# Layer 0 of a two-layer graph network on one core: h2 in a PSUM bank, and the one-hot's transposes in one bank with one copy

## The reference

```python
def _L0_gnn_ref(x, edge_index, W1, b1, W2, b2):
    x_i, x_j = x[dst], x[src]
    msg_in = jnp.concatenate([x_i, x_j - x_i], axis=-1)
    h = jax.nn.leaky_relu(msg_in @ W1 + b1, 0.01)
    h = jax.nn.leaky_relu(h @ W2 + b2, 0.01)
    return jax.ops.segment_sum(h, dst, num_segments=x.shape[0])
...
x = _layernorm(x + _L0_gnn_ref(x, edge_index, ...), axis=-1)
x = _layernorm(x + _L1_gnn_ref(x, edge_index, ...), axis=-1)   # graph attention, 4 heads
```

## Time and profile before

| | |
|---|---|
| median of 3 runs | 8842.36 us (8837.32 to 8854.7) |
| the profiled execution's own time | 8853.59 us |
| its span (first to last instruction) | 8851.8 us |
| busy: PE, PEld, DVE, ACT, POOL | 5979.6, 4612.0, 5775.0, 3918.0, 6098.9 us |
| gathers of layer 0 (3136), first to last start | 87.2 to 4055.2 us |
| gathers of layer 1 (3136), first to last start | 4222.3 to 8582.6 us |
| mean granted clock of TensorE | 0.888 of full |

### The profile page before, as it was taken

The page is one execution under the profiler, slowest core; times in us unless marked ns, Lnnn a source line. Parts: engine busy times, 40 slices in busy tenths (PEclk is TensorE's granted clock), DMA queues, the critical chain, the costliest instruction groups (busy, mean ns, idle before and its releaser), DMA issues.

```text
span 8851.8 us, 202989 instructions
## 1 busy us (share of the span) xinstructions
PE 5979.6 (68%) x46823; PEld 4612.0 (52%) x46824; DVE 5775.0 (65%) x13889; ACT 3918.0 (44%) x10077; POOL 6098.9 (69%) x6281
## 2 busy tenths in 40 slices
PE   4777777777777777776366666666666666666667
PEld 3556555555555555555244445444444444444446
DVE  3555555555555555556477777777777777777776
ACT  3445444544444444444244444444444444444443
POOL 4777777777777777772777776767676766766650
PEclk7889888988988888888698989999898989999897
DMA  3111111111111111112111111111111111111110
GB/s 99 40 40 40 39 40 40 40 40 40 39 40 40 40 40 40 40 40 30 27 29 30 28 28 26 28 27 28 27 27 27 27 28 26 27 28 27 27 21 15
DMA packets 276883, 301.80 MB, mean 34 GB/s; under 512 B 169511, under 2 KB 173108, under 8 KB 276566
## 3 DMA queue, kind: packets, MB, share of 16 engines
q0 software_dynamic: 200704, 265.33, 14.7%
q1 hardware_dynamic: 74082, 32.92, 1.5%
q10 hardware_dynamic: 2068, 3.20, 0.1%
HBM read 286.33 MB, written 16.30 MB: 34 GB/s over the span
## 4 chain that ended last, share of the span: by engine, by line
DVE 25%; issue 22%; POOL 21%; PE 18%; DVEq 6%; ACT 4%; ACTq 2%; POOLq 1%; DMA 1%; SPq 0%
POOL big L382 21%; DVE S L485 8%; PE ps L970 6%; PE pu L956 4%; DVE state L684 2%; DVE rel L482 2%; PE ps L846 2%; DVE rowA L633 1%; DVE rowD L638 1%; POOLq L373 1%; DVE Y L665 1%; DVEq L256 1%; DVEq L700 1%; ACT rowX L1087 1%; ACT ST L1174 1%
## 5 line engine op out<-in xcount | busy, mean ns | idle before, releaser
L382 POOL DMA_INDIRECT big<-x_dram,idx x3136 | 3084.8, 984 | 1442.5 <-issue 892.7
L382 POOL DMA_INDIRECT big<-q_dram,idx x3136 | 3013.0, 961 | 1041.2 <-issue 1033.9
L956 PE MATMUL pu<-Y,S 128*128 128x265 f32 x7856 | 2147.5, 418 | 738.2 <-DVE Y L665 732.5
L956 PEld LDWEIGHTS pu<-Y,S 128*128 128x128 f32 x7856 | 1497.5, 201 | 1030.8 <-issue 782.2
L665 DVE TENSOR_TENSOR Y<-big,ps 128x1040 f32<-128x1040 f32 x982 | 1210.7, 1233 | 659.0 <-ACT ps L1178 572.5
L485 DVE TENSOR_TENSOR S<-ps,rel 128x1024 f32 x978 | 1197.8, 1225 | 222.1 <-DVE rel L482 222.1
L1075 ACT COPY ST<-ps 128x512 bf16<-128x512 bf16 x978 | 538.8, 586 | 1703.7 <-PE ps L846 1703.6
L860 PE MATMUL pu<-rowX,S 128*128 128x192 bf16 x3936 | 578.0, 264 | 980.4 <-issue 718.6
L522 DVE TENSOR_TENSOR Y<-Y,rowX 128x512 f32<-128x512 f32 x491 | 341.7, 696 | 1221.3 <-ACT rowX L1087 1218.9
L860 PEld LDWEIGHTS pu<-rowX,S 128*128 x3936 | 383.7, 98 | 1174.7 <-issue 1063.5
L970 PE MATMUL ps<-identb,S 128*128 128x128 bf16 x3912 | 550.3, 231 | 523.9 <-DVE S L485 522.7
(11 more groups left out here) (176 smaller groups left out, 8322.6 us busy)
## 6 DMA issues: line engine op xcount, KB each, us to landing
big<-q_dram,idx POOLq DMA_INDIRECT x3136
big<-x_dram,idx POOLq DMA_INDIRECT x3136
rowD<-dst_dram SPq DMA_DIRECT2D x196, 32.0 KB
x_dram<-big SPq DMA_DIRECT2D x7, 483.0 KB, 6.1
idx<-srcT_dram SPq DMA_DIRECT2D x98, 32.0 KB, 1.7
dstc<-dstT_dram SPq DMA_DIRECT2D x98, 32.0 KB
q_dram<-state SPq DMA_DIRECT2D x2, 1536.0 KB, 9.6
out<-big SPq DMA_DIRECT2D x6, 448.0 KB
```

Source lines behind the costliest of these rows:

```text
L382: nc.gpsimd.indirect_dma_start(o, None, x_dram if l else q_dram, bass.IndirectOffsetOnAxis(ap=idx[:, half, t:t + 1], axis=0)).then_inc(gat ...
L956: last = t_.matmul(bank, Sf[:, t, :], Y[:, t, :], start=(t == 0), stop=(t == 7))
```

## The change

`h2` becomes the view `ps[1][:, :]`, a whole PSUM bank of 128 x 512 float32, in place of a quarter of `Y`. `h2`, `hi`, `rest`, `mid` and `lo` address it there. To free the bank, the 8 transposes of the one-hot go to `ps[0]` (8 x 128 columns of bf16 fill it), with one pair of semaphores `stp`, `sts` instead of two, and ACT moves them to `ST` in one copy of 128 x 1024 instead of two of 128 x 512. PE waits for the whole copy before z0. DVE gets a wait on its own `lo` ahead of the write of `h2`, and in the prologue a wait for the index rows' copies (`rc`) and one more memset of a bank. Layer 1's turn calls the helper `to_sbuf` for the copy that it had written out.

```diff
--- before.py
+++ after.py
@@ -140,7 +140,7 @@
         h1 = Yf[:, 0:TG * D].rearrange("p (t d) -> p t d", d=D)
         az1 = Yf[:, TG * D:2 * TG * D].rearrange("p (t d) -> p t d", d=D)
         az2 = Yf[:, 2 * TG * D:3 * TG * D]
-        h2 = Yf[:, 3 * TG * D:4 * TG * D]
+        h2 = ps[1][:, :]
         h2p = rowX[:, 0:3 * TG * D // 2].bitcast(bf16).rearrange("p (k c) -> p k c", k=3)
         h1T = rowA[:, 0:4 * P].rearrange("p (t e) -> p t e", e=P)
         Sf = S[:, 2 * TG:4 * TG, :].rearrange("p t n -> p (t n)").bitcast(f32).rearrange("p (t n) -> p t n", n=P)
@@ -164,7 +164,7 @@
         fredge_flatd = sem("fredge_flatd")
         gdone = sem("gdone")
 
-        LAGS = [{"rel": 0, "S": 0, "stp0": 0, "stp1": 0, "sts0": 0, "sts1": 0, "z0": 0, "z1": 0, "az0": 0,
+        LAGS = [{"rel": 0, "S": 0, "stp": 0, "sts": 0, "z0": 0, "z1": 0, "az0": 0,
                  "az1": 0, "h0": 1, "h1": 1, "htp": 1, "hts": 1, "z2": 1, "az2": 1,
                  "h2": 2, "hi": 2, "rest": 2, "mid": 2, "lo": 3, "U": 3, "us": 4, "acc": 4},
                 {"rel": 0, "S": 0, "stp": 0, "sts": 0, "ad": 0, "adx": 1, "zz": 1,
@@ -517,6 +517,7 @@
                                             hv(az1, h), ALU.max).then_inc(m[f"h{h}"], 1)
                     if k.has(2):
                         k.after("az2", 2)
+                        k.after("lo", 3)
                         v.tensor_tensor(h2, ps[7][:, :], az2, ALU.max).then_inc(m["h2"], 1)
                         k.after("hi", 2)
                         v.tensor_tensor(h2, h2, h2p[:, 0, :], ALU.subtract).then_inc(m["rest"], 1)
@@ -533,7 +534,8 @@
 
             prime(dve, 0, "rel S h0 h1 h2 rest lo us acc")
             dve.sem_inc(fredge_flatd, 2)
-            for n in (2, 4, 5, 6, 7):
+            dve.wait_ge(s["rc"], 2 * NU)
+            for n in (1, 2, 4, 5, 6, 7):
                 link(v.memset(ps[n][:, :], 0.0))
             link(v.memset(rowX[:, :], 0.0))
             dve.wait_ge(s["b2in"], 16)
@@ -838,13 +840,12 @@
 
             def transposes(k, buf):
                 k.after("S", 0)
+                k.after("sts", 1)
                 hot = S[:, ds(buf, TG), :]
-                for h in range(2):
-                    k.after(f"sts{h}", 1)
-                    o = ps[h][:, 0:2 * P].bitcast(bf16)
-                    for t in range(4):
-                        last = t_.transpose(o[:, t * P:t * P + P], hot[:, h * 4 + t, :], identb[:, :])
-                    last.then_inc(L[k.l][f"stp{h}"], 1)
+                o = ps[0][:, :].bitcast(bf16)
+                for t in range(TG):
+                    last = t_.transpose(o[:, t * P:t * P + P], hot[:, t, :], identb[:, :])
+                last.then_inc(L[k.l]["stp"], 1)
 
 
             def turn0(half):
@@ -872,8 +873,8 @@
                                                     .rearrange("p t d -> p (t d)"), ident[:, :])
                         last.then_inc(m["htp"], 1)
                     if k.has(0):
+                        k.after("sts", 0)
                         for h in range(2):
-                            k.after(f"sts{h}", 0)
                             for j in range(3):
                                 t_.matmul(ps[4 + h][:, 0:256], identb[:, :],
                                           g0[:, ds(k.r * TG + (half * TS + 4 * h), 4), j, :], start=(j == 0),
@@ -904,7 +905,7 @@
 
             pe.wait_ge(s["b2in"], 16)
             pe.wait_ge(s["idb"], 1)
-            prime(pe, 0, "stp0 stp1 htp z0 z1 U z2")
+            prime(pe, 0, "stp htp z0 z1 U z2")
             pe.sem_inc(gdone, 2)
             pe.wait_ge(clean, 1)
             supers(pe, steps0)
@@ -1070,11 +1071,9 @@
 
             def to_sbuf(k):
 
-                for h in range(2):
-                    k.after(f"stp{h}", 0)
-                    a_.copy(ST[:, h * 4:h * 4 + 4, :],
-                            ps[h][:, 0:2 * P].bitcast(bf16).rearrange("p (t n) -> p t n", t=4)
-                            ).then_inc(L[k.l][f"sts{h}"], 1)
+                k.after("stp", 0)
+                a_.copy(ST[:, :, :], ps[0][:, :].bitcast(bf16).rearrange("p (t n) -> p t n", t=TG)
+                        ).then_inc(L[k.l]["sts"], 1)
 
 
             def turn0(k):
@@ -1106,7 +1105,7 @@
             def steps0(i, q, half):
                 steps(act, 0, i, first0, turn0)
 
-            prime(act, 0, "sts0 sts1 hts az0 az1 az2 hi mid")
+            prime(act, 0, "sts hts az0 az1 az2 hi mid")
             act.wait_ge(clean, 1)
             supers(act, steps0)
             tails(act, 0, turn0)
@@ -1170,9 +1169,7 @@
                     if k.has(1):
                         ends(k, 0, 1)
                     if k.has(0):
-                        k.after("stp", 0)
-                        a_.copy(ST[:, :, :], ps[0][:, :].bitcast(bf16).rearrange("p (t n) -> p t n", t=TG)
-                                ).then_inc(m["sts"], 1)
+                        to_sbuf(k)
                     if k.has(1):
                         k.after("y1", 2)
                         a_.activation(wb[:, :, :], dw[:, :, :], ACT.Exp).then_inc(m["w"], 1)
```

## The result

The changed kernel takes 8792.2 us (median of 6 runs, 8788.54 to 8796.38) against 8842.79 us for the kernel before in the same comparison (6 runs, 8833.76 to 8854.7): ratio **0.9942**, 95% interval 0.9931 to 0.9953, or 50.6 us less. The forecast was 8800 us. The profiled execution took 8796.38 us, with a span of 8794.5 us; it is the one read here.

The account below looks back on a forecast made before the run. POOL's stream of gathers, not the turn, was taken to bound layer 0. Terms -46.2 + 1 + 3.0 = -42 us, against the median of 8842.36 us, gave 8800 us; range 8780 to 8830.

Parts of the forecast that it names:

- What bounds layer 0: In layer 0 POOL issues gathers end to end and PE waits 706.9 us, so only shortening POOL's stream counts.
- Which gathers are held, and by what (-46.2): Layer 0 gathers starting in `lo` or `rest` wait because both inputs lie in SBUF; `h2` in PSUM saves 46.2 us.
- held by the memset: One of the 167 long gathers began in a prologue memset, counted as held by it for 0.15 us.
- Rival A: Layer 0 holds stay, perhaps from `lo`'s bf16 write into `rowX`: 8845 us, or 8843 if only `rest` is cured; chance 0.13.
- New holds in `acc` (+1): Layer 0's L511 keeps two SBUF inputs and may hold more gathers: +1 us, between nothing and 1.6.
- The turn (+0.37): Each layer 0 turn grows 0.37 us: single copy +0.41, `hi` -0.03, `rest` -0.01; hidden except behind the last gather.
- Rival B: Layer 0's turn grows by more than 1.28 us, so compute becomes the pace: 9140 us; chance 0.05.
- `z` feeds `h0` only in the next turn: In layer 0 z0 starts about 0.6 us later, taken as covered, otherwise part of the same 0.4 us.
- +3.0: Eight turns behind layer 0's last gather are uncovered: 8 x 0.37 = +3.0 us, bounds 0 and 8.4.
- the doubling that bounded it: Upper bound for `rest` reading and writing one PSUM bank: as long again, +0.68 us; nothing was taken.
- its rule of 49 us per 0.1 us: Once layer 0's turn grows beyond 1.28 us, each further 0.1 us costs 49 x 10 x 0.1 = 49 us.
- Layer 1: Layer 1 keeps its instructions, its gathers only shifted in phase: 0, with some 5 us either way.

Follow-up runs that it names:

- experiment 6: Changed kernel plus a needless ACT copy every layer 0 turn, in two kernels: small copy (128 x 128) 8790.09 us, full copy (128 x 1024) 9147.46 us.
- experiment 1: Changed kernel with `h2` back in its quarter of `Y`, merged transposes and single copy kept: 8851.79 us, ratio 1.0008 to the kernel before.
- experiment 2: Changed kernel with `rest` writing its result to SBUF, so `lo` alone of the two has two SBUF inputs: 8808.51 us, ratio 0.9962 to the kernel before.
- experiment 3: Changed kernel with `h2` in SBUF and `rest` writing to PSUM, so `rest` alone of the two has two SBUF inputs: 8845.27 us, ratio 0.9996.
- experiment 4: Changed kernel with layer 0's constant row for `S` moved from PSUM to SBUF, giving `S` (1.22 us) two SBUF inputs: 8957.57 us.
- experiment 7: Changed kernel with `usum` moved from SBUF to free columns of PSUM bank 3, so `acc` has one SBUF input: 8790.18 us, ratio 0.9934.
- experiment 8: Unedited repeats: kernel before 13211.68 and 13223.88 us on one chip; on another, kernel before 8836.64 us and changed kernel 8790.84 us.

## Why the prediction was right

*What bounds layer 0.* POOL's stream, not the turn: right. A turn 0.39 us longer was free in experiment 6, one 1.2 us longer cost hundreds of us.

*Which gathers are held, and by what (-46.2).* Right in kind and size: 46.3 us of holds before, 0.9, 0.4 and 0.6 after, in three profiles. Experiments 1 to 4 and 7 show the cause, two SBUF inputs of the DVE instruction, and exclude the merged copy, the place of the output and the operands' type. Two readings of the prediction were off, at no cost to the sum. The first gather is not held by the memset: it takes 1097 to 1100 ns in all 14 profiles, also where the memset was over (experiment 8). And L503, L522 and L511 are not the only instructions with two inputs in SBUF: `rel` (L482, 0.22 us) reads the tiles `dstc` and `blk`, the second as one number per partition, and none of up to 191 gathers that begin in it is held. Rival A had its test in experiment 3: `lo` with its bf16 write into `rowX` and one PSUM input held nothing. The Trainium skill's inference (SBUF — State Buffer, Who interferes with whom) that a `tensor_tensor` leaves descriptor generation alone does not mean that gathers go on beside one: experiment 4 has a hold of up to 1.02 us (1.97 against 0.95). Another sentence of that section, which the prediction did not weigh, is that an instruction with two SBUF inputs contends with a GpSimd instruction that reads SBUF; it fits these holds, if the gather's reading of its indices is that read. No run separates that reading from the rest of the gather.

*New holds in `acc` (+1).* 0.2 us before, 0.9, 0.4 and 0.6 after: right, and too small to be told from nothing in the time.

*The turn (+0.37).* 0.38 in the middle value. The mean, leaving out the 48 longest, which hold the super-steps' starts, grew by 0.50 (6.99 to 7.49). Turns of up to 11 us that ran at a granted clock of 1.00 throughout grew by 0.42 (6.99 to 7.41, 393 and 295 of them), which is near the forecast; turns with some of the low clock in them number 46 before (mean 6.86) and 150 after (7.74) (see *Rival B*). That PE's wait of 0.59 us ahead of z0 is on the path in the short turns, against "`z` feeds `h0` only in the next turn", is a second possible reason, which no run tests. Behind the last gather it came to **+4.9 us instead of +3.0**; the other two profiles of the changed kernel have 68.8 and 66.9 us there, the second of the kernel before 62.6. The mean granted clock of these stretches is 0.89 and 0.85 in the first two profiles.

*PSUM operands.* `hi` and `mid` fell from 622 and 618 to 592 and 585 ns, as taken. `rest`, reading and writing one bank, went from 696 to 700 ns: the doubling that bounded it did not come, nor did the 0.01 us that the prediction took off. `h2` takes 692 instead of 680, `lo` 683 instead of 688. These are means; the middle values of `rest` and `lo` went from 693 and 682 to 700 and 681; the means before hold 68 instructions that waited for a gather (see the last section). By an estimate from the Trainium skill (VectorE: DVE Perf Modes, The TRN2 errata) `rest` and `lo` should have become 65 ns longer each; no row shows it.

*Rival B.* Its mechanism exists and its rule of 49 us per 0.1 us is about what experiment 6 shows, but the change stays under its point. PE's slack at a super-step's start, a mean of 12.8 us before ((706.9 - 94.3) / 48), is 6.2 after ((387.5 - 95.5) / 47). I had taken one row, 13.68, for the mean. The row with the clock at 1.00 in the earlier trace rows lies one turn after the wait, not two. The fall of the clock inside a super-step, which the prediction named and then set aside, did come, in part. From the first turn to the last gather the clock stood at 0.50 (1.2 GHz) for 823 us before and 812 after, but 157 us of that (46 stretches) lay away from PE's waits for gathers before, and 437 us (86 stretches) after. One of them, between about 2059 and 2062 us, begins in a turn in which PE had stood still for 0.43, 0.41 and 0.59 us:

```profile
2056.00:2060.00 4.00, 3.11 (x28) 2.38 (x29) 2.11 (x6) 2.26 (x4) 3.09 (x4) 0.84 0.17 37
2060.00:2064.00 4.00, 3.93 (x33) 2.90 (x30) 2.79 (x7) 1.58 (x4) 3.09 (x4) 0.73 0.22 45
```

Up to the last gather this cost part of the slack, not time. Nothing here shows which of PE's pauses brings the clock down.

*Why 51 and not 42.* What was summed lies between the first gather of layer 0 and the first of layer 1. There the kernel before takes 4135.1 us in both profiles, and the changed one 45.9, 37.7 and 42.1 us less in three: 42 in the mean, as forecast. The first two of these differ mostly by the gathers' 3 ns (7.2 us of stream). What the medians show beyond that lies behind layer 0, and its cause is open. Chance may do for one comparison, whose interval (0.9931 to 0.9953) reaches from 42 to 61 us; but the second (55.2 us) leans the same way, and so do experiments 1 and 3, which take 21.9 and 7.3 us more than the kernel before from first gather to first gather and have medians only 4.7 us above it and 1.9 below. The term of the prediction in question is *Layer 1* (0, with some 5 us either way). Layer 1's gathers took 4360.3 and 4351.4 us before, and 4338.2 to 4353.2 in nine of ten profiles of the kernels that have the merged copy (4372.3 in experiment 4). A gain of some 10 us there is possible, and not shown.

## What to carry to other kernels

Where gathers issued by GpSimd set the pace, look at the longest of them beside the DVE instructions of the moment, not at GpSimd's idle time: a hold is counted as busy. One input of each long DVE instruction in PSUM frees them, at 12 ns or less in the instruction's own length here, and a constant operand is worth a bank for the same reason. A work-saving change elsewhere (here 489 copies) brings nothing that these runs can tell, and a turn may even grow, up to the slack that the waits at a stage's start show; take its mean, not one row.

## What the runs showed of the hardware that I had not expected

**The wait goes both ways.** A gather that begins from 0.02 us before to about 0.03 us after the start of `lo`, `rest` or `acc` is not held; the DVE instruction takes longer instead. In the kernel before 28 `lo` and 40 `rest` lasted more than 20 ns longer than usual for this, up to 0.76 us, with the gather at its usual length:

```profile
306.66 0.75 DVE L503 TENSOR_TENSOR rowX<-Y,rowX 128x512 bf16<-128x512 f32 x1
306.69 0.94 POOL L382 DMA_INDIRECT big<-q_dram,idx  x1 [0.30 <-issue]
```

In the changed kernel no `lo` or `rest` does so. `rel`, which holds no gather, is held by one in another place: when it starts between 0.47 and 0.7 us after a gather does, it ends with that gather, and lasts up to 0.47 us instead of 0.22 (65 of 477 in the changed kernel).

**Layer 1 has more of it, and the change leaves it there.** In the kernel before 486 of its gathers last over 0.967 us, 117 us more than the median in sum, against 46 in layer 0. All 48 that begin in L638, a scan of 2.28 us with two inputs in SBUF, are held, for 69 us; of the 817 that begin in L665, which has one input in PSUM, none is. The first of the 48:

```profile
4308.83 2.28 DVE L638 TENSOR_TENSOR_SCAN rowD<-rowX,rowA 32x1024 f32<-32x1024 f32 x1
...
4309.01 2.94 POOL L382 DMA_INDIRECT big<-x_dram,idx  x1 [0.31 <-issue]
```

What freeing them would bring was not run.

**Phases decide the number.** The number of held gathers hangs on phases so finely that the same kind of instruction, 0.700 or 0.682 us long, held 258 or 82. Much of it repeats from one execution to the next (149 holds in `lo` both times, streams of 3968.0 us both times), and some does not (12 and 18 in `rest`; 24, 11 and 17 in `acc` in three profiles of the changed kernel). A count can't be scaled to another turn length: taking `lo`'s holds away while `rest` kept its two SBUF inputs won nothing (8845 us). The duration of a gather differs by up to 3 ns between executions of one program, and one of the chips ran the kernel before at 13.2 ms, with PE's idle time inside turns given as "issue" and gathers as short as elsewhere (median 947 ns).
